# A graph network's five attention layers: other sizes and steps of the softmax groups, and the join of runs that cross tiles moved beside the last pairs

## The reference

```python
for l in range(5):
    xw = x @ W
    xj = xw[src].reshape(-1, H, D) + edge_emb.reshape(-1, H, D)
    xi = xw[dst].reshape(-1, H, D)
    alpha = leaky_relu(einsum(xi, att_i) + einsum(xj, att_j), 0.2)
    amax = segment_max(alpha, dst); ea = exp(alpha - amax[dst])
    denom = segment_sum(ea, dst)
    alpha = ea / (denom[dst] + EPS)
    aggr = segment_sum(xj * alpha[..., None], dst)
    x = aggr.mean(axis=1) + b          # relu between layers
```

## Time and profile before

| | |
|---|---|
| median of 3 runs | 5361.3 us (5350.91 to 5364.48) |
| the profiled execution | 5359.46 us, span from first to last instruction 5357.6 us |
| TensorE busy | 4321.4 us, 81% |
| VectorE busy | 4012.9 us, 75% |
| ScalarE busy | 3341.6 us, 62% |
| GpSimd busy | 3259.0 us, 61% |
| first memset of the five layers (line 1338) | 1587.9, 1951.6, 2320.1, 2688.5, 3057.0 us |

### The profile page before, as it was taken

The page is one execution under the profiler, slowest core; times in us unless marked ns, Lnnn a source line. Parts: engine busy times, 40 slices in busy tenths (PEclk is TensorE's granted clock), DMA queues, the critical chain, the costliest instruction groups (busy, mean ns, idle before and its releaser), DMA issues. The chain is left out here.

```text
span 5357.6 us, 101824 instructions
## 1 busy us (share of the span) xinstructions
PE 4321.4 (81%) x28013; PEld 3723.5 (69%) x28013; DVE 4012.9 (75%) x15157; ACT 3341.6 (62%) x9065; POOL 3259.0 (61%) x2905
## 2 busy tenths in 40 slices
PE   4899999999967969969969789776995858598575
PEld 4777777778857858858858667544775847476375
DVE  5799999999976757767767767785777959567665
ACT  2788887888846847847858668544773547566300
POOL 2888888878877737457277277124642267465277
PEclk6999999999979979979989889756997979899755
DMA  2998876666635636536456355587664759656232
GB/s 89 191 218 219 222 218 214 220 215 210 210 136 132 137 77 140 129 92 143 103 113 143 86 133 136 150 249 198 149 136 111 199 150 257 176 114 114 57 93 85
DMA packets 1107280, 825.55 MB, mean 154 GB/s; under 512 B 209511, under 2 KB 1068203, under 8 KB 1106397
## 3 DMA queue, kind: packets, MB, share of 16 engines
q1 hardware_dynamic: 1026800, 690.47, 48.1%
q0 software_dynamic: 77040, 128.08, 11.9%
q10 hardware_dynamic: 2880, 0.50, 0.1%
HBM read 374.78 MB, written 448.11 MB: 154 GB/s over the span
## 5 line engine op out<-in xcount | busy, mean ns | idle before, releaser
L805 POOL DMA_INDIRECT gat_G<-table,k_src_row x980 | 1070.2, 1092 | 316.7 <-issue 281.1
L1598 ACT ACTIVATE gat_Gw<-gat_G,gat_al 128x128 f32<-128x128 f32 x1960 | 618.5, 394 | 89.1 <-DVE gat_al L1423 89.1
L1454 DVE SCALAR_TENSOR_TENSOR gat_Gw<-gat_own,gat_al,gat_Gw 128x128 f32<-128x128 f32 x1960 | 554.3, 342 | 70.1 <-ACT gat_Gw L1598 69.9
L1715 PE MATMUL gat_psG<-gat_ends_at,gat_Gw 128*128 128x128 f32 x3920 | 534.8, 280 | 43.1 <-DVE gat_Gw L1454 43.0
L1743 PE MATMUL gat_psZ<-gat_aggT,t_gat_wh 128*128 128x256 f32 x1960 | 527.9, 393 | 15.3 <-ACT gat_hT L1624 14.9
L1715 PEld LDWEIGHTS gat_psG<-gat_ends_at,gat_Gw 128*128 128x128 f32 x3920 | 491.0, 196 | 53.6 <-DVE gat_Gw L1454 50.6
L635 PEld LDWEIGHTS nodes_psR<-t_ident_v,nodes_hTl 128*128 128x128 f32 x3168 | 435.5, 193 | 106.0 <-issue 1.8
L635 PE MATMUL nodes_psR<-t_ident_v,nodes_hTl 128*128 128x132 f32 x3168 | 450.7, 279 | 0.0
L479 POOL TENSOR_TENSOR nodes_rstd<-nodes_var,k_half 128x14 f32<-128x14 f32 x140 | 367.2, 2623 | 116.6 <-DVE nodes_var L546 116.4
L1624 ACT ACTIVATE gat_hT<-gat_psZ,t_gat_bias 128x256 f32<-128x256 f32 x490 | 231.6, 473 | 268.9 <-PE gat_psZ L1744 265.9
L1743 PEld LDWEIGHTS gat_psZ<-gat_aggT,t_gat_wh 128*128 128x128 f32 x1960 | 340.0, 194 | 56.8 <-ACT gat_aggT L1605 17.2
(11 more groups left out here) (668 smaller groups left out, 12604.8 us busy)
## 6 DMA issues: line engine op xcount, KB each, us to landing
table<-nodes_rows SPq DMA_DIRECT2D x660, 198.0 KB
table<-nodes_n SPq DMA_DIRECT2D x396, 192.0 KB
gat_own<-table SPq DMA_DIRECT2D x490, 132.0 KB
table<-gat_rows SPq DMA_DIRECT2D x392, 132.0 KB
nodes_x<-in_x SPq DMA_DIRECT2D x132, 192.0 KB
out<-nodes_x_out SPq DMA_DIRECT2D x132, 192.0 KB
gat_G<-table,k_src_row POOLq DMA_INDIRECT x980
hgt_q<-enter_q SPq DMA_DIRECT2D x98, 144.0 KB, 2.2
```

What stands on the lines that cost most here:

```text
L805: eng.indirect_dma_start(to, None, table, bass.IndirectOffsetOnAxis(ap=index, axis=0)).then_inc(sem, 16)
L1454: ins = eng.scalar_tensor_tensor(Gw[:, i % RS, t, h, :], own[:, i % RO, t, 0:D], al[:, g % 2, 1, a:a + 1], Gw[:, i % RS, t, h, :], ALU.mul ...
L1598: ins = eng.activation(Gw[:, i % RS, t, h, :], G[:, i % RG, t, 0:D], ACT.Copy, scale=al[:, g % 2, 0, a:a + 1])
L1715: mm = eng.matmul(o[:, h * P:(h + 1) * P], Gw[:, i % RS, t, h, :], ends_at[:, i % RE, t, :], start=True, stop=True)
```

## The change

The groups become 10, 11, 12, 13, 13, 13, 13 and 13 pairs, and the four steps of each stand at four pairs in a row. A group's edge bursts are cut evenly instead of 7 and the rest. ScalarE still weighs 4 pairs before its loop. SyncE stores the last group's ends at pair 84 instead of 86 and loads the statistics at pair 85 instead of 89. VectorE's work on the crossing runs is cut in five pieces at pairs 88 to 92, the copies for the join stand at pair 94 and the first join at 96. ScalarE's exp of it comes at pair 88, `carried` at pairs 94 and 95. TensorE turns the weights of the runs at pair 93 instead of 98, sums tiles 0 to 127 at pair 97 and turns the last 68 in the loop's last round.

```diff
-GAT_PAIRS = (4, 12, 14, 14, 14, 14, 14, 12)
-GAT_STEPS = ((1, 2, 3, 3), (8, 9, 11, 11), (9, 10, 12, 13), (8, 9, 11, 12), (6, 8, 10, 11), (5, 7, 9, 10), (5, 7, 9, 10), (0, 0, 0, 0))
+GAT_PAIRS = (10, 11, 12, 13, 13, 13, 13, 13)
+GAT_STEPS = ((6, 7, 8, 9), (7, 8, 9, 10), (8, 9, 10, 11), (8, 9, 10, 11), (7, 8, 9, 10), (6, 7, 8, 9), (5, 6, 7, 8), (0, 0, 0, 0))
...
-        for k in range(0, G.pairs, most):
-            out.append(EdgeBurst(G.first + k, min(most, G.pairs - k), g))
+        parts = (G.pairs + most - 1) // most
+        for k in range(parts):
+            a, b = k * G.pairs // parts, (k + 1) * G.pairs // parts
+            out.append(EdgeBurst(G.first + a, b - a, g))
...
-                            if k == 0:
+                            if k == 0 and g + 1 < NG:
                                 store_ends(g)
-                        if i == NP - 9:
+                            if i == NP - 14:
+                                store_ends(NG - 1)
+                        if i == NP - 13:
                             eng.wait_ge(stats_out, 16 * H * NG)
...
-                    if i == NP - 3:
+                    if i == NP - 10:
+                        runs_top()
                         eng.wait_ge(s.pie_turned, 1)
                         eng.tensor_copy(pr[:, 0, :, :, :].rearrange("p e h d -> p (e h d)"), psT[:, :]).then_inc(s.pr, 1)
-                    if i == NP - 5:
-                        runs_top()
+                    if i == NP - 9:
+                        runs_sums()
+                    if i == NP - 8:
+                        runs_scans()
+                    if i == NP - 7:
+                        runs_inverse()
+                    if i == NP - 6:
+                        runs_weights()
+                    if i == NP - 4:
+                        take_crossing()
                     if i == NP - 2:
-                        runs_sums()
-                    if i == NP - 1:
-                        runs_weights()
+                        join_first()
...
-                weighed_to = groups[0].pairs
+                weighed_to = 4
...
-                    if i == NP - 5:
+                    if i == NP - 10:
                         eng.wait_ge(s.to_exp, NG + 1)
...
-                    if i == NP + 1:
+                    if i == NP - 4:
                         carried(0, P)
+                    if i == NP - 3:
+                        carried(1, C - P)
...
-                    if i == NP - 6:
+                    if i == NP - 12:
                         eng.wait_ge(s.px, P // 2)
...
-                    if i == NP:
+                    if i == NP - 5:
                         eng.wait_ge(s.pr, 1)
...
+                    if i == NP - 1:
+                        sum_first()
+                    if i == NP + 1:
+                        turn_second()
```

More of the change, by code:

```diff
@@ L1499, in runs_weights @@
                     step(eng.reciprocal(AS, W0))
+                def runs_weights():
                     step(eng.tensor_tensor(W0, den, P0, ALU.mult))
@@ L1503, in runs_weights, with take_crossing, join_first @@
                     eng.tensor_tensor(AS, EL, AS, ALU.mult).then_inc(s.weights, 1)
+                def take_crossing():
+                    eng.wait_ge(s.weights_turned, 1)
+                    for n, (a, b) in enumerate(half):
+                        step(eng.tensor_copy(wc[0:b - a, n, :, :].rearrange("p k h -> p (k h)"),
+                                             psT[0:b - a, 2 * E2 + n * 3 * H:2 * E2 + (n + 1) * 3 * H]))
+                    eng.sem_inc(s.wc, 1)
+                    eng.wait_ge(s.zeroed, 1)
+                    step(eng.tensor_copy(diag_heads(prE[:, 0, :, :, :]), psT[:, 0:2 * E2].rearrange("p (e h f) -> p e h f", e=2, h=H)))
+                def join_first():
+                    eng.wait_ge(s.ox_weighed, 1)
+                    eng.wait_ge(s.pr, 1)
+                    for h in range(H):
+                        step(eng.scalar_tensor_tensor(comb[:, 0, h, :], pr[:, 0, 0, h, :], wc[:, 0, 0, h:h + 1], comb[:, 0, h, :], ALU.mult, ALU.add))
+                        step(eng.tensor_scalar(prE[:, 0, 0, h, :], prE[:, 0, 0, h, :], wc[:, 0, 0, h:h + 1], None, ALU.mult))
+                    eng.sem_inc(s.comb, 1)
                 own_scores(0)
@@ L1548, in _ @@
                         next_scores(i - 6)
[L1549 to L1557, removed]
[L1558 to L1561 removed]
                 m = C - P
                 eng.wait_ge(s.pie_turned, 2)
[L1564 removed]
+                step(eng.tensor_copy(diag_heads(prE[0:m, 1, :, :, :]), psE[1][0:m, 0:2 * E2].rearrange("p (e h f) -> p e h f", e=2, h=H)))
                 eng.wait_ge(s.ox_weighed, 2)
@@ L1757, in to_rows, with turn_second, sum_first @@
                     mm.then_inc(s.rowed, 1)
+                def turn_second():
+                    eng.wait_ge(s.px, NP)
+                    eng.wait_ge(s.pe, NB)
+                    eng.wait_ge(s.aggT, NP)
+                    eng.wait_ge(s.aggE, NB)
+                    for e0 in range(2):
+                        for h in range(H):
+                            eng.transpose(psG[1 - e0][0:C - P, h * D:(h + 1) * D], pie[:, h, e0, P:C], K.ident[:, :])
+                        mm = eng.transpose(psE[1][0:C - P, e0 * E2:(e0 + 1) * E2], pieE[:, e0, P:C], K.ident[0:E2, 0:E2])
+                    mm.then_inc(s.pie_turned, 1)
+                def sum_first():
+                    eng.wait_ge(s.comb, 1)
+                    eng.wait_ge(s.cw, 1)
+                    eng.wait_ge(s.aggE, NB)
+                    for h in range(H):
+                        o = psT[:, h * C:(h + 1) * C]
+                        eng.matmul(o, pr[:, 0, 1, h, :], cw[:, 0, h, :], start=(h == 0), stop=False)
+                        eng.matmul(o[:, 0:P], comb[:, 0, h, :], K.ident[:, :], start=False, stop=False)
+                    for h in range(H):
+                        eng.matmul(psE[0][0:E2, 0:C], prE[:, 0, 1, h, :], cw[:, 0, h, :], start=(h == 0), stop=False)
+                    for h in range(H):
+                        eng.matmul(psE[0][0:E2, 0:P], prE[:, 0, 0, h, :], K.ident[:, :], start=False, stop=False)
                 turn_own(0)
```

29 lines of the change are left out of this document (2 added, 27 removed).

## The result

The changed kernel takes 5451.1 us (median of 4 runs, 5447.0 to 5454.0), the kernel before in the same comparison 5357.9 us. The ratio is 1.0174, with a 95% interval of 1.0156 to 1.0191. The forecast was 5421 us in a range of 5375 to 5465: direction and range hold, the size is 30 us short.

The account below looks back on a forecast made before the run. TensorE was taken to bound the pair loop, without slack once the pipeline runs. Per layer 11.3 - 31.5 + 33.3 - 1.0 + 2.8 - 1.4 = +13.5 us, five layers 67.5, less 6: 5421 us, range 5375 to 5465.

Parts of the forecast that it names:

- part 1: First group, grown from 8 tiles to 20: first weighed row at 2355.6 instead of 2344.2, +11.3 us (bounds 10 and 13).
- The stalls for the weights: TensorE's waits for turned weights between groups: 3.0 us in six transitions, 2.0 for group 6, 20.0 us together.
- part 2: Transitions between groups: weights stalls 20.0, second stall 7.9, own scores 5.4, together 33.3 us against 31.5 removed (bounds 11.2 and 38).
- The second stall: ScalarE blocks until take before weighing the next group, delaying mixing: 3 x 2.3 for groups 0 to 2, 1.0 for group 3, 7.9 us.
- The own scores: The next group's own scores hold VectorE before pair 2 of each group: 6 x 0.9 = 5.4 us stay.
- part 3: TensorE's clock: low stretches before cost 5.4 us; 2.0 remains and three transitions lose 1.2 each time, sum -1.0 per layer.
- the clock falls at each transition: Rival on transitions: seven clock falls a layer at 1.7 us instead of three at 1.2, +8.3 per layer, 5462 us; chance 0.17.
- part 4: End of a layer: TensorE gains 1.0 and 0.4 us; VectorE, given the crossing runs' work, falls short by 2.8 (bounds 0 and 6).
- The statistics: SyncE's store and load of the last group's statistics at pairs 84 and 85: VectorE waits 2.1 us for them.
- the 3 us granted there for gather waits: First and last layers: later gather waits leave about 3 us each at TensorE; shorter groups ask for fewer gathers, so -6.
- even steps keep TensorE fed: Rival on transitions: weights ready before TensorE arrives, each costs 1.6 and the clock stays high, -12 per layer, 5293 us; chance 0.09.

Follow-up runs that it names:

- experiment 2: The kernel before with only the weights step of groups 1 to 6 one pair sooner, one pair behind their scores: 5445.6 us, ratio 1.0169.
- the fitted filler: The changed kernel with useless products before the weights waits, 8 in the second group and 12 in later ones: 5426.5 us, ratio 1.0140.
- The fillers: The changed kernel with useless TensorE products ahead of the weights waits: 16 each, 5423.2 us; cut to 8 and then 12, 5426.5 us.
- experiment 3: The changed kernel with useless TensorE products filling the weights waits to keep the clock up: 5423.2 us with 16, 5426.5 us with 8 and 12.
- experiment 5: Here: the changed kernel with two pairs between scores and weights, its new join one pair later throughout: 5346.5 us, ratio 0.9987.
- the version with the old join: New groups and edge pieces, source, scores and weights two pairs apart, join at its old place: 5325.8 us, ratio 0.9951 against the kernel before.
- the first group's experiment: The kernel before with a first group of 10 pairs, others 12 or 13, scores and weights two pairs apart, even edge pieces: 5385.1 us, ratio 1.0056.

## Why the prediction was right, and where not

- **The start** (part 1). Forecast: first weighed row at 35.6 us, +11.3 in the third layer. Measured 2399.48 - 2364.1 = 35.4, first eviction +11.2. Right. In the first layer, where I let a longer wait for group 1 cancel 4 us, the first eviction is 15.4 later and its first group gives 13.0 back where the third's gives 12.7: that cancelling didn't take place.
- **The stalls for the weights** (part 2). Forecast 20.0 us after the first pair, measured 20.1: 2.03, four of 2.92, 3.01 and 3.37. The five middle ones are right, and the earlier trace rows plus one pitch was the way to them; experiment 2 shows that the step is the cause. That the sum fits to 0.1 is partly luck, two errors of about 1 us that cancel. The 2.0 was meant for group 6 with its edge burst, and that transition takes 3.37: the burst also delays the mixing and the evictions that stand ahead of the exp in ScalarE's queue, so that the exp starts 0.1 us before the aggregate ends (2667.97 and 2668.10), where it is 0.5 in the transition of group 5 shown above. The 2.03 stands in the first transition, where TensorE had itself waited 0.62 us for VectorE's rows.
- **The second stall** (part 2). Forecast 7.9, measured 3.7. ScalarE is idle for 5.63, 4.79, 4.80 and 4.77 us before it weighs groups 1 to 4, as foreseen. With the fitted filler, at the full clock, TensorE's wait for hT is 7.6 us (2.82, 1.98, 1.99, 0.79), and 3.7 at the low clock: the forecast was right for a clock that wasn't there. It had summed two things of which one hides the other.
- **The own scores**. 0.9 at the third pair of each of six groups, as forecast.
- **The clock** (part 3), the term that was mis-sized. Forecast -1.0 per layer, with 2.4 for falls in three transitions, 12 us in five layers. The profile shows a fall in five of the seven transitions of the third layer, in all seven of the first, where six are twice as long; TensorE's work at 0.50 is 175.8 us in the five layers against 93.9. The fillers put these falls at 18 to 28 us. So the rival "the clock falls at each transition" described the mechanism better than the forecast did (its 5462 us is 11 away, 5421 is 30), but at 8.3 us per layer its price was too high for the middle layers, for the reason in experiment 3. A row of the first layer at the low clock:

```profile
1774.10:1780.50 6.40, 6.06 (x21) 5.39 (x22) 6.40 (x26) 3.82 (x12) 2.83 (x1) 0.50 0.13 33
```

- **The end** (part 4), the second term. Forecast 2.8 - 1.4 = +1.4 per layer, measured 3.1 + 0.8 = 3.9 in the third. Where and how TensorE waits was right, at pairs 90 to 93, 0.69 + 0.29 + 0.69 + 0.52 = 2.2 us, in place of 2.8. Two things were missing. With the new groups the last group costs 1.2 more over the pitch even with the old join (4.5 for 3.3). And the tail doesn't shrink. Its last products run at the low clock, and the two that answer to each other take 1.25 us in place of 0.72 (changed, then before); how much of the tail's 2.2 us that makes in all was not taken apart:

```profile
2741.58 1.25 PE L1871 MATMUL gat_psR<-t_ident_v,gat_hTx 128*128 128x132 f32 x4 [0.51 <-ACT gat_hTx L1701]
```
```profile
2680.88 0.72 PE L1843 MATMUL gat_psR<-t_ident_v,gat_hTx 128*128 128x132 f32 x4 [0.51 <-ACT gat_hTx L1681]
```

- **The statistics.** VectorE waits 3.52 us for them instead of the 2.1 forecast; SyncE and VectorE show why:

```profile
2686.78 1.62 SPq L1301 DMA_DIRECT2D stats<-gat_ends  x2
...
2692.82 0.85 SPq L1337 DMA_DIRECT2D gat_st<-stats  x3
...
2694.84 0.96 DVE L1486 TENSOR_TENSOR_SCAN gat_wt<-k_q_restart,gat_st 2x392 f32<-2x392 f32 x1 [3.52 <-DMA gat_st<-stats]
```

The load is used 2.0 us after its issue began, but the store's landing lets SyncE on only 4.4 us after its issue ended; I had taken one price for both. The 2.0 us of the Trainium skill, DMA: Bandwidth & Descriptors, section Anatomy of one DMA, is given there for transfers that GpSimd issues, and these are SyncE's; the load agrees with it and this store doesn't. What the wait costs stays open: in experiment 5 it went and others came in its place.
- **The sum.** Third layer 17.5 for 13.5: start -0.1, first group and transitions with the clock +1.6 (2.4 for 0.8), end +2.5. First layer 27.7 for about 10.5: the start 4.1 more than forecast, first group and transitions with the clock 6.9, the end 3.1, and the 3 us granted there for gather waits didn't come. The last layer, with what follows it, is 13.4 us longer; whether the 3 us granted to it are in that isn't shown.
- **The rival on the other side** ("even steps keep TensorE fed", 5293 us) named its condition rightly: the exponential must end a pair earlier. With that condition met by the steps, the changed kernel takes 5336 us and the version with the old join 5326, so its time was 33 us or more too low. Part of that is its sum, which takes -4.4 for the clock where part 3's own numbers give -5.4 + 2.0 = -3.4 (5 us in five layers).

What stays open: why most low stretches of the first layer are twice as long as in the second and third behind the same stalls, how much of the first group's experiment (+30 us) belongs to the edge pieces, and how the price of the join divides into work and waits of VectorE.

## What to carry to other kernels

Where one engine goes through its queue in order and needs the end of a chain that runs over others, compare the chain's length with the number of work units between its two steps: here 3.1 us in one unit of 2.64 lost 92 us, in two units it cost almost nothing, and a third brought nothing. A low clock behind a stall is paid only where the engine would not have waited for another a moment later, so a sum must not add both. Work that leaves the tail for a stage whose bound it doesn't touch still has to fit into the lead of the engine that does it.

## What the runs showed of the hardware

- In the second to fourth layer of the changed kernel a stall of 2.92 us on TensorE is followed by 3.4 us at 0.50 in ten cases of twelve, beginning 0.8 to 1.6 us after the stall's end (2509.67 and 2511.2 in the transition shown). In the other two, 2.92 and then 1.98 us in group 1 of the second and third layer, it stays at 1.00. With 2.8 us of useless products in the same gap it stays up in most transitions, in the first layer in all.
- A stretch of 3.4 us at the low clock costs 1.6 us in one transition and nothing in another.
- An fp32 product of 128 x 128 takes 0.23 to 0.24 us at 2.4 GHz and shows as two records (24 in 2.84 us for 12 products, 3.74 us for 16).
- A store of the statistics let its waiter on 4.4 us after its issue, a load of the same data was used 1.2 us after its own had ended.
